# Kernel of eight layers: key fills moved to GpSimd, value products in one piece, four heads per step at the end of attention, recurrence in wider operations

## The reference, cut to what matters

```python
Q, K, V = (x @ W.T for W in (W_Q, W_K, W_V))                 # per head: HD = 8
attn = Q @ K.T / sqrt(HD) + slopes * min(pos_k - pos_q, 0)   # causal, softmax over keys
x = layernorm(x + (softmax(attn) @ V) @ W_O.T)
...
h = diag_lambda * h + Bu_t                                   # complex, 512 positions, 4 sequences
out = (hs * C_complex).real + inputs * D_skip
```

## Time and profile before

| | |
|---|---|
| runs | 1303.97, 1304.48, 1309.03 us |
| profiled execution | 1310.25 us, its span 1308.5 us |
| TensorE matmul busy | 1096.4 us (84%) |
| VectorE busy | 800.7 us (61%) |
| ScalarE busy | 546.6 us (42%) |
| GpSimd busy | 378.3 us (29%) |
| granted TensorE clock, mean | 0.893 |

### The profile page before, as it was taken

One profiled execution on the slowest core, in us unless ns is written; L12 is line 12 of the kernel. 1 busy time (PEld: TensorE's weight loads), 2 busy tenths in 40 slices (PEclk: granted clock), 3 DMA queues, 4 the chain that ended last, 5 costly groups with the idle time before them and its releaser, 6 DMA issues. The chain is left out here.

```text
span 1308.5 us, 29552 instructions
## 1 busy us (share of the span) xinstructions
PE 1096.4 (84%) x9991; PEld 808.5 (62%) x9999; DVE 800.7 (61%) x2758; ACT 546.6 (42%) x1207; POOL 378.3 (29%) x515
## 2 busy tenths in 40 slices
PE   8999887784998884799977768886788989899892
PEld 4666655674466851556645325553776979889792
DVE  5566255344588868645677874556953757757424
ACT  4366642474544322222223122323123746648483
POOL 2344406343100620000000115540034434524442
PEclk9899988998998566799998877998978999999997
DMA  1210449222000059079743255544902212032222
GB/s 46 51 41 4 145 160 372 63 64 77 1 2 3 5 190 336 1 160 184 288 172 137 86 180 132 141 97 155 297 13 72 66 35 67 21 71 46 56 53 66
DMA packets 112948, 135.94 MB, mean 104 GB/s; under 512 B 16948, under 2 KB 78471, under 8 KB 112145
## 3 DMA queue, kind: packets, MB, share of 16 engines
q1 hardware_dynamic: 100208, 119.26, 30.1%
q0 software_dynamic: 12592, 14.79, 4.5%
HBM read 67.92 MB, written 69.32 MB: 105 GB/s over the span
## 5 line engine op out<-in xcount | busy, mean ns | idle before, releaser
L2204 PE MATMUL m_psY<-large,m_hT 128*128 (+2 forms) x992 | 139.2, 284 | 0.0
L2204 PEld LDWEIGHTS m_psY<-large,m_hT 128*128 128x128 f32 x992 | 126.7, 191 | 0.1
L2124 POOL DMA_INDIRECT rows<-m_ys,m_slot x93 | 90.7, 975 | 116.5 <-DVE m_slot L2360 107.1
L626 DVE TENSOR_REDUCE at_peaks<-at_ps 128x3 f32<-128x384 f32 x128 | 65.4, 551 | 45.9 <-PE at_ps L389 45.9
L538 ACT ACTIVATE at_PT<-at_ps,at_bias 128x384 f32<-128x384 f32 x128 | 67.3, 577 | 48.0 <-PE at_ps L399 47.9
L2260 ACT ACTIVATE m_hT<-m_psH 128x512 f32<-128x512 f32 x124 | 73.7, 594 | 30.1 <-PE m_psH L2186 29.7
L331 POOL TENSOR_SCALAR_AFFINE_SELECT at_PT<-at_PT 128x256 f32<-128x256 f32 x128 | 54.8, 430 | 72.0 <-ACT at_PT L538 68.1
L1515 POOL IOTA row_no<- 128x1 f32 x1 | 0.1, 132 | 251.2 <-SPq L744 251.2
L2186 PE MATMUL m_psH<-m_xT,large 128*128 128x128 f32 x512 | 67.6, 275 | 0.0
L2272 ACT ACTIVATE m_ys<-m_psY,m_weight 128x144 f32<-128x144 f32 x124 | 47.3, 381 | 42.8 <-PE m_psY L2204 38.2
L2186 PE MATMUL m_psH<-m_xT,m_up 128*128 128x128 f32 x480 | 63.6, 276 | 0.0
(11 more groups left out here) (738 smaller groups left out, 2806.0 us busy)
## 6 DMA issues: line engine op xcount, KB each, us to landing
rows<-blank SPq DMA_DIRECT2D x16, 2448.0 KB, 21.3
m_xs<-rows SPq DMA_DIRECT2D x124, 76.5 KB, 2.0
pair_rows<-blank SPq DMA_DIRECT2D x1, 8320.0 KB, 26.1
large<-in_L_attn_firs SPq DMA_DIRECT2D x4, 2048.0 KB, 18.9
large<-comb_rows SPq DMA_DIRECT2D x64, 128.0 KB, 5.8
se_wu<-in_L_ffn_up SPq DMA_DIRECT2D x32, 192.0 KB, 2.6
W2T<-in_L_ffn_down_turned SPq DMA_DIRECT2D x1, 4096.0 KB, 12.5
large<-in_L_ffn_up SPq DMA_DIRECT2D x4, 1024.0 KB, 8.6
```

Of the source, the lines that this page charges most:

```text
L626: nc.vector.tensor_reduce(peaks[:, b % 2, n, :], psS[:, u % TILES, 0:CAUSAL].rearrange("p (x c) -> p x c", c=P), AX.X, ALU.max).then_inc(r ...
L2124: pool.indirect_dma_start(k.rows[(layer + 1) % 2], bass.IndirectOffsetOnAxis(slot[:, q:q + 1], 0), ys[:, q, :], None, bounds_check=E3 * N ...
L2204: m = nc.tensor.matmul(psY[b][:, 0:wide], hT[b][:, c * P:(c + 1) * P], w, start=(c == 0), stop=(c == C - 1))
```

## The change

It does six things. (1) VectorE's four fills of `KA` move to GpSimd. (2) The value products move from ahead of head 16 to ahead of head 18, behind the turning of batch 0's maxima, and ScalarE copies these maxima first. (3) The sync queue sends batch 0's maxima after 8 of the 16 row DMAs instead of after all. (4) The maxima of batches 1 to 7 are turned in two pieces into unused columns of the banks of heads v = 16b - 8 and 16b - 7; ScalarE copies each piece ahead of that head's exponential. (5) The last 26 heads go four per step over six banks (three of them freed by pass one), and the projection, the addition and the statistics of three of the four groups are made between them; only group 3 stays in `project_and_add_stage`. (6) In the recurrence real and imaginary parts lie side by side and 12 VectorE operations of 512 columns become 6 of 1024.

```diff
-    BEFORE = {0: range(0, 14), 2: range(14, 16), 4: range(16, 18), 16: range(18, 22)}
+    BEFORE = {0: range(0, 14), 2: range(14, 16), 4: range(16, 18), 18: range(18, 22)}
+    ALONE = ALL - LEAD
+    RING = TRING + TILES - 1
...
+            def dots_bank(v):
+                if v < ALONE:
+                    return psT[:, v % TRING, :]
+                r = (v - ALONE) % RING
+                return psT[:, (ALONE + r) % TRING, :] if r < TRING else psS[:, r - TRING, :]
+            piece_of = {HEADS * (b + 1) + 2 - LEAD + half: (b, half) for b in range(1, BATCH) for half in range(2)}
...
                 for g in range(GROUPS):
+                    if g == 2:
+                        send_peaks(0)
...
+                pool.wait_ge(*ready.at(4))
+                for g in range(GROUPS):
+                    nc.gpsimd.tensor_scalar(KA[:, g, 512:N].rearrange("p (b n) -> p b n", n=SEQ),
+                                            k.at_const[:].unsqueeze(1).to_broadcast([P, BATCH - 2, SEQ]),
+                                            k.at_slope[:, g:g + 1], None, ALU.mult).then_inc(keys_filled.sem, 1)
                 pool.wait_ge(*keys_filled.at(4))
...
+                def turn_peaks(v):
+                    b, half = piece_of[v]
                     pe.wait_ge(*peaked.at(b + 1))
+                    nc.tensor.matmul(dots_bank(v)[0:HEADS, CAUSAL:CAUSAL + P], peak1[:, b % 2, :] if half else peaks[:, b % 2, :, 0],
+                                     minus[:], start=True, stop=True, skip_group_check=True)
...
+                FIRST, LAST = ALONE // TILES, QUADS - 1
+                quad_of = lambda q: range(TILES * q, TILES * q + TILES)
+                dots_alone(range(ALONE, TILES * (FIRST + 1)))
+                weigh_both(FIRST - 1)
+                turn_outputs(0)
+                dots_alone(quad_of(LAST - 5))
+                weigh_both(FIRST)
+                project_outputs(0)
+                dots_alone(quad_of(LAST - 4))
+                weigh_both(LAST - 5)
+                turn_outputs(1)
+                pe.wait_ge(*peak_in[(BATCH - 1) % 2].at(64 * BATCH // 2))
+                dots_alone(quad_of(LAST - 3))
+                weigh_both(LAST - 4)
+                project_outputs(1)
...
+                weigh_both(LAST)
+                turn_raw(BATCH - 1)
...
                 for v in range(ALL):
                     act.wait_ge(*dotted.at(v + 1))
+                    if v in piece_of:
+                        copy_peaks(v)
...
+                def copy_and_add(g):
+                    dve.wait_ge(*o_turned.at(g + 1))
+                    nc.vector.tensor_copy(QT[:, g * 512:(g + 1) * 512], psP).then_inc(o_copied.sem, 1)
+                    dve.wait_ge(*o_projected.at(g + 1))
+                    x = k.X[:, 4 * g:4 * g + 4, :]
+                    nc.vector.tensor_tensor(x, x, psP.rearrange("p (t d) -> p t d", d=D), ALU.add).then_inc(added.sem, 1)
+                    gather_stats(k, dve, x_stats, range(4 * g, 4 * g + 4))
...
+        project_and_add_stage(k, "at", O, QT, wo, groups=(3,))
...
+                nc.vector.tensor_tensor(m[:, 0], b2[:, b], waves(1), ALU.mult)
+                nc.vector.tensor_tensor(m[:, 1], b2[:, b], waves(0), ALU.mult).then_inc(turned_back.sem, 1)
+                dve.drain()
+                nc.vector.tensor_tensor(turned_in[:], m[:, :, 0], m[:, :, 1], ALU.add)
+                dve.drain()
+                nc.vector.tensor_tensor_scan(four(state[:]), flat(w["decay"][:]), four(turned_in[:]), 0.0, ALU.mult, ALU.add)
...
+                for i in range(2):
+                    nc.vector.tensor_tensor(parts[:, b, 2 * i:2 * i + 2], state[:], waves(i + 1), ALU.mult)\
+                        .then_inc(parted.sem, 2)
```

168 lines of the change are left out of this document (103 added, 65 removed).

## The result

The changed kernel takes 1297.22 us (median of 7 executions, 1292.37 to 1302.88) against 1305.58 us of the kernel before beside it: a ratio of 0.9939, 95% interval 0.9915 to 0.9964, so 0.6% faster. A second series of 12 gave 1297.27 us and 0.9955, 0.9927 to 0.9984. Forecast were 1292.8 us and faster, with 1285 to 1300 as the range: the sign and this range hold, the narrower one of 1288 to 1297 is just missed, and the time came out 4.4 us above the forecast. By the sum of its terms -11.7 us were expected, and the two comparisons show some -6 to -8.

What follows compares the result with a forecast made beforehand. Attention was taken as bound by TensorE, late for maxima and a halved clock at the start and for ScalarE at the end. Terms -6.2 + 2.4 - 2.8 - 3.9 - 1.2 = -11.7 us from 1304.48 gave 1292.8; range 1285 to 1300.

Steps and rivals of the forecast that it cites:

- The second of them: Rival: the median run has no clock fall at the start, which gives only -1.2 us; time 1297.8, chance 0.17.
- start: First part of attention: wait and clock fall go, pass two starts near 44.2 instead of 50.38, -6.2 us.
- middle: Steps where peaks are turned: turning products and copies stand in front, 0.4 us a batch, six batches, +2.4 us.
- end phase: Last heads of pass two, four per step: 22 us instead of 24.9, -2.8 us, bounds -4.9 and 0.
- projection: Block behind attention, only group 3 left: 8.9 us instead of 12.8, -3.9 us, ending on TensorE's warming.
- recurrence: Wider VectorE operations save 1.7 us of fixed parts, TensorE waits 0.5 us longer: -1.2 us.
- the clock falls elsewhere: Rival: the new end phase's wait of about 1 us may halve the clock, costing 3 to 4 us; 1297, chance 0.20.
- VectorE's first weighting of the values stays among these heads: Start of attention: the reason given why nothing beyond -6.2 us can be gained there.
- If the maxima's DMAs end pass two's wait at the start: Sign of failure: batch 0's maxima landing late for pass two; three to four us of room were expected, so 0.
- nothing beyond -6.2: Bound on the gain at the start of attention; the other bound was -1.2 us if the clock falls all the same.
- Four fills, 10.3 us: Start: GpSimd's moved fills at 2.6 us each, free from 7.5 us on, ending before 20.
- Late fills: Rival: fills of 4 us and more on GpSimd make key DMAs land after head 32 wants them; 1296, chance 0.03.

Runs made afterwards that it cites:

- the experiment with the old turning: Changed kernel with the maxima of batches 1 to 7 turned as in the kernel before; middle 84.87 us, end phase 23.79 us instead of 22.4.
- the run with two warming products: Changed kernel with two warming products instead of five ending the last group's projection; last turning to norm 8.48 us, against 12.71 in its second run.
- the doubled fills: Changed kernel with GpSimd doing its four fills twice, 16.6 us of added work; single execution, TensorE waits 2.21 us for keys at head 32.

## Why the prediction was right, and where it was off

Sign and range are right, but that owes something to luck. The terms gave 4.9 to 7.8 us of the 11.7, and the range of 1285 to 1300 holds the time because it was drawn wide for two rivals. Both had the time almost exactly (1297 and 1297.8). The second of them, that the median execution has no fall at the start, had it by chance: both traces with the old order show the fall.

Times at the norm behind attention or of the last pair's products, us; the second column is the first trace of the changed kernel, the third the second one, whose start kept its clock.

| term | forecast | first trace | second trace |
|---|---|---|---|
| start, to the ninth head (forecast: to pass two's start) | -6.2 | -1.9 | -5.5 |
| middle | +2.4 | +2.24 | +2.2 |
| end phase | -2.8 | -2.74 | -2.75 |
| projection | -3.9 | -1.4 | -0.7 |
| attention, sum | -10.5 | -3.8 | -6.7 |
| recurrence, to the last products | -1.2 | -1.1 | -1.1 |

*The start* was right in what it gives and wrong in what it sets off. "The wait and the fall" do go, and the value products take the 3.84 us that the prediction took from the projection. Pass two started at 44.55 in the second trace where 44.2 was said, and at 45.24 in the first. But the step "VectorE's first weighting of the values stays among these heads" took it to cost nothing new. Its waits of 0.47 and 0.17 us stood at the same place before, without a fall behind them. With the new order they stand there too, and in 5 of the 8 traces that have both the clock falls to 0.50 by 48 us, which costs 2.0 to 3.5 us between pass two's start and the ninth head (9.24 to 10.75 us where it takes 7.22 at full clock). With the weighting two heads earlier it fell in none of four. That speaks for these waits as a condition of the fall but does not prove it: five falls in twelve traces would miss a given four in about 1 case of 14. The rival "the clock falls elsewhere" had the mechanism and about the price (3 to 4 us), but looked for it in the end phase. In these 8 traces it is rather the rule than a chance of 0.20. The DMA wait of 1.21 us, which I had put at 0, is real but comes and goes; by the prediction's own sign ("If the maxima's DMAs end pass two's wait at the start") the forecast fails there in the first trace. The bound "nothing beyond -6.2" holds only for the table as it is: with the weighting moved pass two started at 42.79, 7.6 us earlier than before.

*The moved fills* were mis-sized without harm. "Four fills, 10.3 us" were 16.62 us and ended at 25.80, not before 20, and the key DMAs started at 26.50 behind the last key copy, as said. The rival "Late fills" had its condition met (more than 4 us a fill) and not its consequence.

*The middle* held, 2.24 us against 2.4, and the experiment with the old turning shows that its two causes together are all of it (another 0.3 us, of the turning ahead of the ninth head, is in the start's row). The term should have been a warning: it is a cost without a purpose outside the end phase, and leaving it out there is worth its full size.

*The end phase* held within 0.1 us. The wait for batch 7's maxima, expected at 1 us, did not show. The wait for GpSimd's mask at the tail is 1.12 us, 0.3 us longer than before (0.80 us at 165.74).

*The projection* is the failed term. The forecast's mechanism was right, with TensorE's warming as the end of the block and VectorE's additions long done. But the sum "0.96 for four products, then the five warming products, 4.4 us" took prices from a block that ran at full clock. TensorE is busy for 1.72 of the 4 us from 162 to 166 us in the first trace, and the clock is at 0.50 when the last group comes, in all eight traces with this projection: 2.08 us for products of 0.96, and 5.0 to 6.6 us for the warming. Of 3.9 us 1.4 and 0.7 came in the two traces of the table, and 0.7 to 2.4 over the eight. Nor was the full clock of the old block assured: the trace with the end phase undone has 0.50 in it. I had also named some 2 us that VectorE would allow; it was 3.6 us in the first trace (3.88 less the barrier) and 4.2 in the run with two warming products, against the second.

*The recurrence* held, in the pair (8.40 us) and in the sum. The 0.07 us taken for the fixed part of an operation holds too: in the kernel before, products of 512 columns start 0.60 to 0.61 us apart, and one of 1024 is followed after 1.14, which is 0.06 to 0.08 less than twice that.

The median is 4.4 us above the forecast. The projection falls short by 2.5 to 3.2 us and the start by 0.7 to 4.3, and the two are enough for it: the comparisons show 6 to 8 us where the terms of the two traces add up to 4.9 to 7.8, so no further cause is needed, though at this spread none is excluded. Why the untouched layer takes 181.6 or 190.2 us is left open. The time at which it starts does not settle it, since 182.5 and 189.0 us began 0.2 us apart.

## What to carry to other kernels

A price read at full clock may not hold where the work around it changes. Where a change takes work out of a tail, take the tail's own products at the lower level too, and ask which warming now ends the block. When a wait is removed, look for the next one on the same engine: here the first fall went with one reduction's wait and a new one came near the next, and a table entry took that wait out of the way. A scheme made for one phase, here the turning in pieces, should be tried in that phase alone. Where the layers behind differ by several microseconds from one execution to the next, read a part of the change at a mark of its own and in more than one trace.

## What the runs showed of the hardware

- Whether the clock fell at the start of pass two differed between executions of one kernel. In four of the five traces with the fall the value products began at 33.80 to 34.53 us, in the three with the same waits and no fall at 34.82 to 34.89. The fifth, with the doubled fills, began at 34.95 and had a wait of 1.17 us. What decides is open: the same waits did both.
- A fill of 128x1536 by GpSimd, one input with a scalar from a pointer, takes 16.62 / 4 = 4.15 us, where VectorE took 1.01; the masking of 256 columns that I scaled from (430 ns) gives 2.6.
- While GpSimd filled, VectorE's weighting of the values, which reads two operands from SBUF, took 2.05 us instead of 1.35, and TensorE's wait for the maxima behind it was 1.17 us instead of 0.47. VectorE's reductions, which read PSUM, stayed at 1.02. VectorE's timeline of the run with doubled fills:

```profile
40.01 1.02 DVE L719 TENSOR_REDUCE at_peaks<-at_ps 128x3 f32<-128x384 f32 x2 [4.73 <-PE at_ps L415]
40.95 2.05 DVE L694 TENSOR_TENSOR large<-large,at_weight 128x1152 f32<-128x1152 f32 x1
```

  The Trainium skill (GPSIMD Engine Reference, Specifications) says that GpSimd shares its SBUF interfaces with VectorE and contends with instructions that read two SBUF inputs; this trace agrees. In the change as it stands the fills end at 25.80 us, before the first such operation.
